# Pre-LN attention and mixture-of-experts block: value projection and second half of routing moved, scores, maxima and exponentials ahead of gate, up and tanh in each step

## The chip, the cores and the metric

One core of a Trainium2 chip. The metric is device time in microseconds (us), here the median of 3 runs. All engines of the core take part: PE (TensorE), ACT (ScalarE), DVE (VectorE), POOL (GpSimd) and SP (SyncE, which only issues DMAs).

## What is computed

A transformer block on x of 32 sequences x 256 tokens x 128 channels in fp32. Below, the reference cut to what matters.

```python
x = x + attn(layernorm(x))            # 16 heads of 8; a query at i sees keys i-63 .. i
x = x + ffn(layernorm(x))
# ffn, per token, 16 experts of 64 hidden, 4 groups of 4 experts:
scores = sigmoid(x @ gate_kernel) + gate_bias
group_sum = sum of the two best scores of each group; the best 2 groups are kept
topk_weight, topk_idx = top_k(where(group kept, scores, 0), 4)
topk_weight = topk_weight / (sum(topk_weight) + 1e-20) * 2.5
y = sum over the 4 experts of weight * ((silu(x @ w_gate) * (x @ w_up)) @ w_down)
shared = (silu(x @ sw_gate) * (x @ sw_up)) @ sw_down      # 128 hidden
return y + shared
```

## The kernel before

The 8192 tokens go through in 16 groups of 512 tokens (two sequences of 256, `GB` = 2). The program is a pipeline written out by hand. Time is cut into slots of 8 steps (`STEPS`); a slot is one new group. Every piece of work has a stage number: stage d of group g runs in slot g + d // 8, step d % 8. So stage 28 (`FF`) of group g runs three slots and 4 steps after its LN1. The function `at` says whether a stage falls into a step. Slots 0 to 5 and 16 to 19 are unrolled, slots 6 to 15 run in a loop, two slots per turn.

Each engine has its own instruction list: for each step, the pieces that fall into it, in an order fixed by the code. Engines meet only at semaphores. Nothing reorders the list of an engine but this code.

In a slot in the middle of the run, work of five groups is under way at once:

- Attention. LN1 (stage 0), transposes of x (`XT` 1), Q projection (`QP` 2), V projection (`VP` 3), K projections of the two sequences (`KP` 6, 8). Q and K exist as a high and a low fp32r part; ACT makes the high parts (`q_hi`, `k_hi`), POOL the low parts (`q_lo`, `k_lo`), DVE the differences (`xT_lo`, `qr_lo`, `kr_lo`, `x_lo`). `v_bd` is V laid out by heads, by ACT (`VB` 4, 5).
- Scores (`SC` 8 to 15): PE writes a unit in two halves to PSUM banks 0 and 1 (band mask L979, products L986); DVE takes the negative maximum of each half (`neg_max` L805); ACT makes the exponentials (`probs` L604, eight instructions); in the next step DVE transposes them (`probsT` L754, stage `TR` 9); PE multiplies with V (`PV` 11, L918) into bank 2, ACT copies that out (`o_f`, stage `OE` 14 and 18), PE transposes (`OT`), DVE divides (`o_n` L819), PE transposes again (`ON`), ACT copies (`oT`), PE applies Wo (`OW`), DVE adds x (`H2`).
- LN2 (17, 21), transposes (`XT2`), router logits (`LG` 24). Routing is shared by POOL and DVE: POOL sums pairs of scores (`pair`, step 0), DVE takes group maxima and the two best groups (`gs`, `g8`, `g_out`, `g_in`, step 1), POOL masks the scores (`ms`, step 1), DVE takes the best experts (`m8`, `w_sum`, `m_out`, step 2), POOL makes the weights (`comb`, step 2). PE transposes them in step 3 (`CT` 27), ACT copies `cT`, SP sends them to DRAM and reads them back spread over partitions (`spread`).
- Feed-forward (`FF` 28 to 35, one pair of experts k per step): PE makes gate into bank 4 and up into bank 5 (`gate_up`, lines L876 to L878); ACT makes tanh of the gate (`th` L562) and a copy of it (`gate`); DVE `tu` = (tanh + 1) * up (L793); POOL gate * spread (L468) and `hh` (L471); PE the down projection a step later (`DN` 29, L1060). `gate_up` of the next pair waits for `tu` and for the gate copy, since banks 4 and 5 are used again. The shared expert (`SH` 27, step 3) uses the same banks after pair 7; its tanh is L580, DVE's `fa` L835 and `hs` L839.

PSUM banks 3 and 6 are a ring of two (`RING`) for all projections and transposes: each use takes the next bank and PE waits until the use before the last one has been taken out. The order of the uses follows from the stage numbers and the places EARLY, POST, WEIGHTS, LATE in a step.

The order inside a step before, cut to the two threads:

```python
# PE:   PV, [K0], [V], [LG], FF gate_up(k), SC scores(u), OT, ON, OW, CT, SH, ..., DN
# ACT:  o_f, kr_hi, th_r, FF th(k), gate(k), oT, cT, SH th, late copies, SC exponentials(u), q_hi, k_hi, v_bd
# DVE:  probsT(u-1), [routing 0], [V], OUT, kr_lo, LN1, [routing 1], FF tu(k), [routing 2, 3],
#       max(u) half 0, [routing 4], max(u) half 1, [routing 5], LN2, o_n, H2, SH fa, hs, [routing 6], low parts
```

## Time and profile before

| | us |
|---|---|
| median of 3 runs | 883.22 |
| lowest, highest | 879.14, 885.05 |
| profiled execution, its own time | 882.66 |
| its span in the profile | 880.9 |
| PE busy | 764.8 |
| POOL busy | 616.3 |
| ACT busy | 607.9 |
| DVE busy | 548.1 |

The profiled execution's own time is 1.8 us longer than its span: start and end lie around it. Busy shares are means over filling, the steady middle and draining; a slot can be found in the trace by its LN1 instruction (`ve` L429 on POOL, 16 times). In a timeline row the first number is the start in us from the span's start, the second the duration in us, then engine, line, operation, output<-inputs, xcount of merged instructions, and in brackets how long the engine was idle before and what ended that. The granted clock is TensorE's, 1.00 for 2.4 GHz and 0.50 for 1.2 GHz.

### The profile page before, as it was taken

The page shows a single profiled execution, that of the slowest core. Times are in us where ns is not written, and L with a number is a line of the kernel's source. Part 1 is how long each engine was busy: PE and PEld are TensorE (multiplying, and loading weights), DVE is VectorE, ACT ScalarE, POOL GpSimd, SP SyncE. Part 2 cuts the span into 40 slices and gives each one's busy share as a digit, 9 for nine tenths or more (in the row PEclk, how much of TensorE's full clock was granted, in tenths as well). Part 3 has the DMA queues.
Part 4 walks back from the last instruction along what each step waited for, and adds up shares of the span by engine and source line. Part 5 has one row for each costly group of instructions (what it writes and reads, how often), then busy time and mean ns, then how long its engine had stood idle before and what let it go on. Part 6 is the DMA issues. An engine that isn't in the chain of part 4 may idle for free.

```text
span 880.9 us, 19798 instructions
## 1 busy us (share of the span) xinstructions
PE 764.8 (87%) x5984; PEld 623.5 (71%) x5984; DVE 548.1 (62%) x1751; ACT 607.9 (69%) x1816; POOL 616.3 (70%) x825
## 2 busy tenths in 40 slices
PE   2567789898998989898998989899898989998876
PEld 1455667686877868687787868678786868777665
DVE  3456666767676676767676676766758676664341
ACT  5678677686767768686876868677677868764332
POOL 2525457778686767968686787868677786857666
PEclk9789799999999999999999999999999999999999
DMA  5000022030312103031312204031211303030321
GB/s 143 24 2 25 1 74 61 17 116 15 99 49 86 61 23 124 0 105 40 97 48 64 81 2 119 24 97 48 82 63 31 114 0 105 29 106 29 122 81 42
DMA packets 50738, 53.86 MB, mean 61 GB/s; under 512 B 5632, under 2 KB 31744, under 8 KB 50560
## 3 DMA queue, kind: packets, MB, share of 16 engines
q1 hardware_dynamic: 50688, 53.25, 19.8%
q8 instruction: 24, 0.39, 0.2%
q14 instruction: 26, 0.21, 0.1%
HBM read 44.31 MB, written 4.72 MB: 56 GB/s over the span
## 4 chain that ended last, share of the span: by engine, by line
PE 26%; ACT 21%; issue 21%; DVE 15%; POOL 12%; DMA 2%; POOLq 1%; DVEq 1%; SPq 1%; ACTq 0%
ACT probs L604 10%; POOL gate L468 5%; PE PS L876 5%; PE PS L986 4%; PE PS L878 4%; PE PS L877 4%; ACT v_bd L522 4%; DVE probsT L754 3%; DVE neg_max L805 3%; PE PS L1060 3%; ACT q_hi L522 3%; POOL hh L471 2%; POOL k_lo L460 2%; PE PS L918 2%; ACT th L562 2%
## 5 line engine op out<-in xcount | busy, mean ns | idle before, releaser
L604 ACT ACTIVATE probs<-PS,neg_max 128x96 f32<-128x96 f32 (+1 forms) x1024 | 244.4, 355 | 86.5 <-DVE neg_max L805 86.5
L468 POOL TENSOR_TENSOR gate<-gate,spread 128x512 f32<-128x512 f32 x128 | 163.6, 1278 | 137.9 <-DMA spread<-weights_by_expert 69.3
L754 DVE STREAM_TRANSPOSE probsT<-probs 128x384 f32<-128x384 f32 (+1 forms) x256 | 124.1, 523 | 113.9 <-ACT probs L604 113.9
L471 POOL TENSOR_TENSOR hh<-gate,tu 128x512 f32<-128x512 f32 x128 | 164.4, 1284 | 15.5 <-POOL gate L468 10.4
L1060 PE MATMUL PS<-wd,hh 128*128 128x128 f32 x1024 | 137.0, 277 | 9.7 <-POOL hh L471 9.7
L793 DVE SCALAR_TENSOR_TENSOR tu<-th,PS 128x512 f32<-128x512 f32 x128 | 87.8, 686 | 84.5 <-PE PS L878 58.7
L1060 PEld LDWEIGHTS PS<-wd,hh 128*128 128x128 f32 x1024 | 127.4, 193 | 15.4 <-POOL hh L471 9.8
L876 PE MATMUL PS<-x_hi,w_hi 128*128 128x512 f32 x288 | 130.3, 453 | 4.8 <-DVE tu L793 3.5
L805 DVE TENSOR_REDUCE neg_max<-PS 128x4 f32<-128x384 f32 (+1 forms) x256 | 124.0, 514 | 9.4 <-PE PS L986 7.1
L562 ACT ACTIVATE th<-PS 128x512 f32<-128x512 f32 x128 | 79.5, 621 | 57.7 <-PE PS L878 57.5
L878 PE MATMUL PS<-x_lo,w_hi 128*128 128x512 f32 x288 | 118.6, 412 | 0.0
L877 PE MATMUL PS<-x_hi,w_lo 128*128 128x512 f32 x288 | 118.3, 411 | 0.0
L918 PE MATMUL PS<-probsT,v_bd 128*64 128x96 f32 (+2 forms) x2048 | 107.7, 248 | 0.3 <-DVE probsT L754 0.3
L986 PE MATMUL PS<-k_hi,q_hi 128*128 128x384 f32 (+2 forms) x256 | 107.2, 419 | 0.0
L979 PE MATMUL PS<-band,ident 128*128 128x256 bf16 (+1 forms) x256 | 73.6, 288 | 30.1 <-POOL k_lo L460 12.4
L918 PEld LDWEIGHTS PS<-probsT,v_bd 128*64 128x64 f32 x2048 | 85.7, 139 | 17.9 <-issue 3.2
L460 POOL TENSOR_TENSOR k_lo<-kr_lo,cst 128x256 fp32r<-128x256 f32 x128 | 74.6, 615 | 21.9 <-DVE kr_lo L661 21.9
L450 POOL TENSOR_TENSOR q_lo<-qr_lo,cst 128x256 fp32r<-128x256 f32 x128 | 75.8, 615 | 17.5 <-PE PS L986 11.9
L986 PE MATMUL PS<-k_hi,q_lo 128*128 128x384 f32 (+2 forms) x256 | 85.7, 335 | 0.0
L979 PEld LDWEIGHTS PS<-band,ident 128*128 128x128 bf16 x256 | 25.4, 99 | 85.0 <-issue 63.1
L986 PE MATMUL PS<-k_lo,q_hi 128*128 128x384 f32 (+2 forms) x256 | 85.5, 334 | 0.0
L522 ACT ACTIVATE gate<-PS 128x512 f32<-128x512 f32 x128 | 79.6, 622 | 0.0
(107 smaller groups left out, 1394.2 us busy)
## 6 DMA issues: line engine op xcount, KB each, us to landing
spread<-weights_by_expert SPq DMA_DIRECT2D x256, 128.0 KB, 3.0
X<-x SPq DMA_DIRECT2D x32, 256.0 KB, 3.5
OUT<-H SPq DMA_DIRECT2D x16, 256.0 KB, 3.0
out<-OUT SPq DMA_DIRECT2D x16, 256.0 KB, 3.2
probsT<-w_gu SPq DMA_DIRECT2D x1, 1152.0 KB, 7.8
wd<-w_down SPq DMA_DIRECT2D x1, 512.0 KB, 8.1
weights_by_expert<-cT SPq DMA_DIRECT2D x16, 32.0 KB, 1.6
probsT<-w_att SPq DMA_DIRECT2D x1, 264.0 KB, 3.4
```

Source lines behind the costliest of these rows:

```text
L468: tt(gate2[:, :], gate[:, k % 2, :], spread[:, k % SP_BUFS, :], ALU.mult).then_inc(s_g2, 1)
L471: tt(hh[:, k % 2, :], gate2[:, :], tu[:, k % 2, :], ALU.mult).then_inc(s_h, 1)
L522: return nc.scalar.activation(dst, src, ACT.Copy, **kw)
L604: ins = nc.scalar.activation(probs[:, u % 2, tt, a, j0:KW], PS[:, tt, a * KW + j0:a * KW + KW], ACT.Exp, bias=neg_max[:, tt, a:a + 1])
L754: ins = v_.transpose(probsT[:, b, :, t0 + tt, c0:3, :].rearrange("p g c q -> p g (c q)"), probs[:, u % 2, tt, :, c0 * Q:KW])
L805: v_.tensor_reduce(neg_max[:, tt, :], src[:, :, j0:KW], AX_X, ALU.max, negate=True).then_inc(s_m, 1)
L876: mm(dst, l_hi, r_hi, start=True, stop=False)
L877: mm(dst, l_lo, r_hi, start=False, stop=False)
L878: return mm(dst, l_hi, r_lo, start=False, stop=True)
L918: ins = mm(PS[r0:r0 + 64, 2, c0:c0 + Q * nq], v_bd[:, g.par, b * NQ + kb, a, :, :].rearrange("p k f -> p (k f)"), pt[:, 3 * kb + 2:3 * kb ...
L986: ins = mm(dst[:, :, KW - nk:KW], ql[:, q1 // Q - 1, :, :].rearrange("p v q -> p (v q)"), kl[:, :, q1 - nk:q1], start=False, stop=(kl is k ...
L1060: ins = mm(PS[:, 7, r], hh[:, k % 2, r], wd[:, k, :], start=(k == 0 and n == 0), stop=(k == NP - 1), skip_group_check=True)
```

## The change

Four things are done.

1. The V projection goes from step 3 to step 5 (`VP` 5), the `v_bd` copies to steps 6 and 7 (`VB` 6), the low K parts of the second sequence on POOL from step 2 to step 3 (`KC_LOW`). The copy of `o_f` stands at the end of ACT's step before (`OE` 13) and not at the beginning of the step.
2. The second half of routing: the eight-best instruction `m8` stands between the two maxima of step 2 (place 4) and not at the beginning of that step, the rest behind `o_n` (places 6 and 7).
3. The group mask: `match_replace` writes -2^60 for a chosen group, and POOL subtracts (`g_in` = `gs` - `g_out`), where DVE compared by a `tensor_scalar`. The kept scores are thus multiplied by 2^60, and so is their sum, to which a constant first column of `m8` adds the small term that a `tensor_scalar` added.
4. In every step PE issues the scores ahead of gate and up, ACT the exponentials ahead of tanh and gate copy, DVE the maxima ahead of `tu`.

```diff
@@ -41,15 +41,16 @@
 
 LN1 = 0
 XT = 1
-QP, VP, VB = 2, 3, 4
+QP, VP, VB = 2, 5, 6
 QC = (4, 8)
 QC_LOW = (4, 9)
 KP = (6, 8)
 KC = (7, 10)
+KC_LOW = (7, 11)
 SC = 8
 TR = 9
 PV = 11
-OE = 14
+OE = 13
 OT, ON, OW = 14, 15, 16
 LN2 = 17
 XT2 = 19
@@ -144,8 +145,8 @@
 LOADS, FFN_LOADS = 4, 4
 PREPARE = 4
 ORDER_PER_SLOT = 5
-ROUTING_DVE, ROUTING_POOL = 9, 4
-NO_SCORE, CHOSEN = -3.0e38, 3.0e38
+ROUTING_DVE, ROUTING_POOL = 8, 5
+NO_SCORE, GROUP_IN = -3.0e38, 2.0 ** 60
...
         ms = sb("ms", [P, NT, E + 4])
-        m8 = sb("m8", [P, NT, 8])
+        m8 = sb("m8", [P, NT, 9])
         m_out = sb("m_out", [P, NT, E + 4])
...
-            pool.wait_ge(s_pool, 4)
+            nc.gpsimd.memset(m8[:, :, 0:1], 2e-20 * GROUP_IN).then_inc(s_pool, 1)
+            pool.wait_ge(s_pool, 5)
...
                     for b in range(GB):
-                        g, _ = at(sl, s, KC[b])
+                        g, _ = at(sl, s, KC_LOW[b])
                         if g:
...
                     if g and part == 1:
-                        pool.wait_ge(s_rt, g.n * ROUTING_DVE + 5)
+                        pool.wait_ge(s_rt, g.n * ROUTING_DVE + 4)
+                        tt(g_in[:, :, :], gs[:, :, 0:N_GROUP], g_out[:, :, 0:N_GROUP], ALU.subtract).then_inc(s_rp, 1)
+                        pool.wait_ge(s_rp, n0 + 3)
                         tt(ms[:, :, 0:E].rearrange("p n (g e) -> p n g e", e=4),
                            sc3.rearrange("p n (g e) -> p n g e", e=4),
                            g_in[:, :, :].unsqueeze(3).broadcast_to([P, NT, N_GROUP, 4]), ALU.mult).then_inc(s_rp, 1)
                     if g and part == 2:
-                        pool.wait_ge(s_rt, g.n * ROUTING_DVE + 9)
+                        pool.wait_ge(s_rt, g.n * ROUTING_DVE + 8)
                         tt(kept[:, :, :], ms[:, :, 0:E], m_out[:, :, 0:E], ALU.subtract).then_inc(s_rp, 1)
-                        pool.wait_ge(s_rp, n0 + 4)
+                        pool.wait_ge(s_rp, n0 + 5)
                         tt(comb[:, :, :], kept[:, :, :], w_sum[:, :].unsqueeze(2).broadcast_to(full),
                            ALU.mult).then_inc(s_cb, 1)
...
-                    g, b = at(sl, s, OE, 4, GB)
-                    if g:
-                        act.wait_ge(s_o_ps, g.n * GB + b + 1)
-                        copy(o_f[:, :, :], PS[:, 2, :].rearrange("p (j q) -> p j q", j=2)).then_inc(s_o, 1)
-
-
...
                                              scale=0.5).then_inc(s_taken[side], 1)
-                    g, k = at(sl, s, FF, 1, NP)
-                    if g:
-                        act.wait_ge(s_g, g.n * NF + k + 2)
-                        nc.scalar.activation(th[:, :], PS[:, 4, :], ACT.Tanh, scale=0.5).then_inc(s_th, 1)
-                        copy(gate[:, k % 2, :], PS[:, 4, :]).then_inc(s_gate, 1)
-
...
                     g, u = at(sl, s, SC, 1, NU)
                     if g:
...
                             ins.then_inc(s_p, 1)
+                    g, k = at(sl, s, FF, 1, NP)
+                    if g:
+                        act.wait_ge(s_g, g.n * NF + k + 2)
+                        nc.scalar.activation(th[:, :], PS[:, 4, :], ACT.Tanh, scale=0.5).then_inc(s_th, 1)
+                        copy(gate[:, k % 2, :], PS[:, 4, :]).then_inc(s_gate, 1)
...
+                    g, b = at(sl, s, OE, 4, GB)
+                    if g:
+                        act.wait_ge(s_o_ps, g.n * GB + b + 1)
+                        copy(o_f[:, :, :], PS[:, 2, :].rearrange("p (j q) -> p j q", j=2)).then_inc(s_o, 1)
                     for b in range(GB):
                         g, pair_ = at(sl, s, QC[b], 1, 2)
...
                     for n in range(NT):
-                        ins = v_.match_replace(g_out[:, n, :], g8[:, n, :], gs[:, n, :], CHOSEN)
+                        ins = v_.match_replace(g_out[:, n, :], g8[:, n, :], gs[:, n, :], -GROUP_IN)
                     ins.then_inc(s_rt, 1)
-                elif half == 0 and place == 6:
-                    dve.wait_ge(s_rt, n0 + 4)
-                    v_.tensor_scalar(g_in[:, :, :], g_out[:, :, 0:N_GROUP], CHOSEN, None,
-                                     ALU.is_ge).then_inc(s_rt, 1)
-
-                elif half == 1 and place == 0:
-                    dve.wait_ge(s_rp, g.n * ROUTING_POOL + 3)
+
+                elif half == 1 and place == 4:
+                    dve.wait_ge(s_rp, g.n * ROUTING_POOL + 4)
                     v_.memset(holder[:, :], 0.0)
                     for n in range(NT):
-                        ins = v_.max(m8[:, n, :], ms[:, n, 0:E])
+                        ins = v_.max(m8[:, n, 1:9], ms[:, n, 0:E])
                     ins.then_inc(s_rt, 1)
-                elif half == 1 and place == 1:
+                elif half == 1 and place == 6:
+                    dve.wait_ge(s_rt, n0 + 5)
+                    v_.tensor_reduce(w_sum[:, :], m8[:, :, 0:1 + TOP_K], AX_X, ALU.add)
+                    v_.memset(m8[:, :, 1 + TOP_K:9], NO_SCORE).then_inc(s_rt, 1)
+                elif half == 1 and place == 7:
                     dve.wait_ge(s_rt, n0 + 6)
-                    v_.tensor_reduce(w_sum[:, :], m8[:, :, 0:TOP_K], AX_X, ALU.add)
-                    v_.memset(m8[:, :, TOP_K:8], NO_SCORE).then_inc(s_rt, 1)
-                elif half == 1 and place == 2:
-                    dve.wait_ge(s_rt, n0 + 7)
-                    v_.tensor_scalar(w_sum[:, :], w_sum[:, :], 2e-20, None, ALU.add)
+                    v_.memset(holder[:, :], 0.0)
                     for n in range(NT):
-                        ins = v_.match_replace(m_out[:, n, :], m8[:, n, :], ms[:, n, :], 0.0)
+                        ins = v_.match_replace(m_out[:, n, :], m8[:, n, 1:9], ms[:, n, :], 0.0)
                     ins.then_inc(s_rt, 1)
-                elif half == 1 and place == 3:
-                    dve.wait_ge(s_rt, n0 + 8)
                     v_.reciprocal(w_sum[:, :], w_sum[:, :]).then_inc(s_rt, 1)
...
                                 probs[:, u % 2, tt, :, c0 * Q:KW])
                         ins.then_inc(s_pt, 1)
 
-                    routing(sl, s, 0)
-
...
                         stats(sl, X[:, g.par, :, :], NT, st1, mv1).then_inc(s_mv1, 1)
-                    routing(sl, s, 1)
-                    g, k = at(sl, s, FF, 1, NP)
-                    if g:
-                        dve.wait_ge(s_th, g.n * NF + k + 2)
-                        dve.wait_ge(s_u, g.n * NF + k + 2)
-                        v_.scalar_tensor_tensor(tu[:, k % 2, :], th[:, :], 1.0, PS[:, 5, :], ALU.add,
-                                                ALU.mult).then_inc(s_tu, 1)
                     routing(sl, s, 2)
                     routing(sl, s, 3)
                     g, u = at(sl, s, SC, 1, NU)
...
                         routing(sl, s, 4 + tt)
+                    g, k = at(sl, s, FF, 1, NP)
+                    if g:
+                        dve.wait_ge(s_th, g.n * NF + k + 2)
+                        dve.wait_ge(s_u, g.n * NF + k + 2)
+                        v_.scalar_tensor_tensor(tu[:, k % 2, :], th[:, :], 1.0, PS[:, 5, :], ALU.add,
+                                                ALU.mult).then_inc(s_tu, 1)
                     g, b = at(sl, s, LN2, 4, GB)
                     if g:
...
                                          ALU.mult).then_inc(s_taken[side], 1)
+                    routing(sl, s, 6)
                     g, b = at(sl, s, OW, 4, GB)
                     if g:
                         side, bank = filled(dve, sl, s, POST)
...
                                          X2[:, g.par, 2 * b:2 * b + 2, :], ALU.add).then_inc(s_taken[side], 1)
+                    routing(sl, s, 7)
                     g, _ = at(sl, s, SH)
                     if g:
                         f = g.n * NF + 1
...
                                                 ALU.mult).then_inc(s_tu, 1)
-                    routing(sl, s, 6)
-
                     keys(1)
...
                         ins.then_inc(s_filled[side], 1)
-
-                    g, k = at(sl, s, FF, 1, NP)
-                    if g:
-                        gate_up(g, k, k + 1)
 
                     g, u = at(sl, s, SC, 1, NU)
...
                             ins.then_inc(s_s, 1)
 
+                    g, k = at(sl, s, FF, 1, NP)
+                    if g:
+                        gate_up(g, k, k + 1)
+
                     g, b = at(sl, s, OT, 4, GB)
                     if g:
                         side, bank = free(POST)
```

The rest of the diff on ACT is the block from the tanh of `FF` to the copies of `XT2`, moved as it is behind the exponentials.

Where the rows of the program stand now. All rows below are from slot 16, where they stand without register instructions between them; the slots before have the same order and, in steps 0 to 3, also LN1 and the projections of a new group. First ACT, step 1 to the beginning of step 2, before: `th` and `gate` are tanh and copy of the gate, `probs` the exponentials.

```order
L562 ACTIVATE th<-PS 128x512
L522 ACTIVATE gate<-PS 128x512
L604 ACTIVATE probs<-PS,neg_max 128x96 x8
L522 ACTIVATE q_hi<-qr_hi,cst 128x8x32 x2
L522 ACTIVATE o_f<-PS 128x512
L562 ACTIVATE th<-PS 128x512
```

ACT at the same place now:

```order
L565 ACTIVATE probs<-PS,neg_max 128x96 x8
L572 ACTIVATE th<-PS 128x512
L526 ACTIVATE gate<-PS 128x512
L526 ACTIVATE o_f<-PS 128x512
L526 ACTIVATE q_hi<-qr_hi,cst 128x8x32 x2
L565 ACTIVATE probs<-PS,neg_max 128x96 x8
L572 ACTIVATE th<-PS 128x512
```

Tanh and gate copy of a step stood ahead of its exponentials and now stand behind them; `o_f` stands ahead of the `q_hi` copies. Next DVE, step 2, before: `m` and `w_sum` are routing, `tu` the feed-forward, `neg_max` the maxima.

```order
L754 STREAM_TRANSPOSE probsT<-probs 128x4x96 x2
L710 MEMSET holder 128x1
L712 MAX m<-ms 128x8 x4
L716 TENSOR_REDUCE w_sum<-m 128x4
L717 MEMSET m 128x4x4
L793 SCALAR_TENSOR_TENSOR tu<-th,PS 128x512
L720 TENSOR_SCALAR w_sum<-w_sum 128x4
L722 MATCH_REPLACE m_out<-m,ms 128x20 x4
L726 RECIPROCAL w_sum<-w_sum 128x4
L805 TENSOR_REDUCE neg_max<-PS 128x4 x2
L818 RECIPROCAL o_rs<-PS 128x32
L819 TENSOR_TENSOR o_n<-PS,o_rs 128x256
```

DVE, step 2, now:

```order
L750 STREAM_TRANSPOSE probsT<-probs 128x4x96 x2
L792 TENSOR_REDUCE neg_max<-PS 128x4
L708 MEMSET holder 128x1
L710 MAX m<-ms 128x8 x4
L792 TENSOR_REDUCE neg_max<-PS 128x4
L799 SCALAR_TENSOR_TENSOR tu<-th,PS 128x512
L811 RECIPROCAL o_rs<-PS 128x32
L812 TENSOR_TENSOR o_n<-PS,o_rs 128x256
L714 TENSOR_REDUCE w_sum<-m 128x4
L715 MEMSET m 128x4x4
L718 MEMSET holder 128x1
L720 MATCH_REPLACE m_out<-m,ms 128x20 x4
```

The maxima moved ahead of `tu` with `m` between them, the rest of routing moved behind `o_n`, and the `tensor_scalar` of `w_sum` is gone.

## Rows read from the trace of the kernel before

**Rows 1.** The page, busy us (share) xinstructions, and the chain by engine.

```profile
PE 764.8 (87%) x5984; PEld 623.5 (71%) x5984; DVE 548.1 (62%) x1751; ACT 607.9 (69%) x1816; POOL 616.3 (70%) x825
PE 26%; ACT 21%; issue 21%; DVE 15%; POOL 12%; DMA 2%; POOLq 1%; DVEq 1%; SPq 1%; ACTq 0%
```

**Rows 2.** Timeline, POOL, the first LN1 instruction of slots 4 and 15.

```profile
147.52 0.20 POOL L429 TENSOR_TENSOR ve<-mv,eps 128x4 f32<-128x4 f32 x1 [2.50 <-DVE mv L675]
...
703.10 0.20 POOL L429 TENSOR_TENSOR ve<-mv,eps 128x4 f32<-128x4 f32 x1 [2.47 <-DVE mv L675]
```

**Rows 3.** Stretches: length, busy PE, PEld, DVE, ACT, POOL, clock, DMA, GB/s.

```profile
350.73:401.52 50.79, 46.87 (x376) 38.49 (x376) 34.23 (x109) 37.38 (x114) 38.42 (x52) 0.97 0.20 62
401.52:450.73 49.21, 45.29 (x376) 37.50 (x376) 33.96 (x109) 37.38 (x114) 38.45 (x51) 1.00 0.21 65
366.00:368.20 2.20, 0.00 (x0) 0.00 (x0) 2.12 (x9) 1.14 (x6) 2.20 (x4) 1.00 0.00 0
369.60:372.60 3.00, 3.00 (x11) 1.98 (x9) 1.78 (x4) 1.99 (x5) 1.94 (x4) 0.50 0.00 0
```

**Rows 4.** Waits over the whole span: us in total, times, longest us.

```profile
DVE probsT L754 <- ACT probs L604: 113.9, 116, 2.1
ACT probs L604 <- DVE neg_max L805: 86.5, 74, 3.0
POOL gate L468 <- DMA spread<-weights_by_expert: 69.3, 16, 6.0
...
PE PS L876 <- DVE o_n L819: 36.5, 13, 3.0
```

**Rows 5.** Timeline, ACT and DVE, an ordinary step, and the spacing of `probsT`.

```profile
419.82 1.04 DVE L754 STREAM_TRANSPOSE probsT<-probs 128x384 f32<-128x384 f32 x2 [0.25 <-ACT probs L604]
...
420.78 0.67 DVE L766 STREAM_TRANSPOSE v_keys<-PS 128x512 f32<-128x512 f32 x1
...
433.04 0.64 ACT L562 ACTIVATE th<-PS 128x512 f32<-128x512 f32 x1
...
433.71 0.69 DVE L793 SCALAR_TENSOR_TENSOR tu<-th,PS 128x512 f32<-128x512 f32 x1 [1.16 <-ACT th L562]
...
434.32 1.01 DVE L805 TENSOR_REDUCE neg_max<-PS 128x4 f32<-128x384 f32 x2
434.90 1.96 ACT L604 ACTIVATE probs<-PS,neg_max 128x96 f32<-128x96 f32 x8 [0.74 <-DVE neg_max L805]
...
436.71 0.95 ACT L522 ACTIVATE q_hi<-qr_hi,cst 128x256 fp32r<-128x256 f32 x2
```

**Rows 6.** Timeline, steps 0 to 3 of slot 9: LN1, routing, V projection, shared expert.

```profile
401.52 0.20 POOL L429 TENSOR_TENSOR ve<-mv,eps 128x4 f32<-128x4 f32 x1 [2.47 <-DVE mv L675]
...
404.76 1.30 POOL L468 TENSOR_TENSOR gate<-gate,spread 128x512 f32<-128x512 f32 x1
...
407.46 0.32 POOL L498 TENSOR_TENSOR sc<-th_r,bias 128x64 f32<-128x64 f32 x1
...
408.54 0.25 DVE L686 TENSOR_REDUCE gs<-pair 128x16 f32<-128x96 f32 x1 [1.20 <-POOL pair L503]
...
412.30 0.20 POOL L477 TENSOR_TENSOR ve<-mv,eps 128x2 f32<-128x2 f32 x1
...
414.39 0.30 POOL L506 TENSOR_TENSOR ms<-sc,g_in 128x64 f32<-128x64 f32 x1
...
419.03 0.50 PE L876 MATMUL PS<-xT_hi,w_hi 128*128 128x512 f32 x1 [2.90 <-DVE o_n L819]
...
423.11 0.48 PE L876 MATMUL PS<-x_hi,w_hi 128*128 128x512 f32 x1
...
424.72 0.69 DVE L835 SCALAR_TENSOR_TENSOR fa<-th,PS 128x512 f32<-128x512 f32 x1 [1.21 <-ACT th L580]
```

**Rows 7.** The two `tensor_scalar` lines: duration in ns min/median/max, first and last start.

```profile
L705 DVE TENSOR_SCALAR g_in<-g_out x16: 142/1044/1058, 109.4 to 839.6; 128x16 f32<-128x16 f32 x16
L720 DVE TENSOR_SCALAR w_sum<-w_sum x16: 161/529/569, 112.7 to 842.2; 128x4 f32<-128x4 f32 x16
```

More of the change, by code:

```diff
@@ L423, in slot @@
                                                 ALU.add).then_inc(s_pool, 1)
-                        pool.wait_ge(s_pool, 5)
+                        pool.wait_ge(s_pool, 6)
                     g, _ = at(sl, s, LN1)
@@ L558, in slot @@
                                              scale=0.5).then_inc(s_taken[side], 1)
+                    g, u = at(sl, s, SC, 1, NU)
+                    if g:
+                        j0 = Q if u % 4 == 0 else 0
+                        if u >= 2 or not (g.fixed and g.n == 0):
+                            act.wait_ge(s_pt, g.n * NU + u - 1)
+                        for tt in range(2):
+                            act.wait_ge(s_m, 2 * (g.n * NU + u) + tt + 1)
+                            for a in range(HG):
+                                ins = nc.scalar.activation(
+                                    probs[:, u % 2, tt, a, j0:KW], PS[:, tt, a * KW + j0:a * KW + KW], ACT.Exp,
+                                    bias=neg_max[:, tt, a:a + 1])
+                            ins.then_inc(s_p, 1)
                     g, k = at(sl, s, FF, 1, NP)
@@ L595, in slot @@
                         copy(x2_hi[:, g.par, T * b:T * b + T], bank[:, 0:T]).then_inc(s_high[side], 1)
-                    g, u = at(sl, s, SC, 1, NU)
+                    g, b = at(sl, s, OE, 4, GB)
                     if g:
-                        j0 = Q if u % 4 == 0 else 0
-                        if u >= 2 or not (g.fixed and g.n == 0):
-                            act.wait_ge(s_pt, g.n * NU + u - 1)
-                        for tt in range(2):
-                            act.wait_ge(s_m, 2 * (g.n * NU + u) + tt + 1)
-                            for a in range(HG):
-                                ins = nc.scalar.activation(
-                                    probs[:, u % 2, tt, a, j0:KW], PS[:, tt, a * KW + j0:a * KW + KW], ACT.Exp,
-                                    bias=neg_max[:, tt, a:a + 1])
-                            ins.then_inc(s_p, 1)
+                        act.wait_ge(s_o_ps, g.n * GB + b + 1)
+                        copy(o_f[:, :, :], PS[:, 2, :].rearrange("p (j q) -> p j q", j=2)).then_inc(s_o, 1)
                     for b in range(GB):
```

## The prediction, made before the changed kernel ran

> **What bounds the kernel now.** I read the page's busy shares and chain first: TensorE (PE) is busy 87% of the span, yet the chain that ended last spends only 26% on it and hops between PE, ACT, DVE and POOL [rows 1]. So no engine is full; hand-overs set the pace. Next, how long one slot (8 steps, 512 tokens) takes: the first LN1 instruction of slot 4 starts at 147.52, that of slot 15 at 703.10 [rows 2], 555.6 us for 11 slots, 50.5 us each. Two neighbouring slots by stretches [rows 3]: one of 50.79 us with a granted clock of 0.97, one of 49.21 with 1.00; PE is busy 46.87 and 45.29, DVE only 34, POOL 38, ACT 37. The difference, 1.58 us, is a stretch at a granted clock of 0.5 (1.2 GHz instead of 2.4), which most slots have: the one shown, 369.6 to 372.6, comes right behind one in which PE did nothing, 366.0 to 368.2. The table of waits says who waits [rows 4]: PE's V projection for `o_n` 36.5 us in 13 times, so 2.9 per slot; DVE's `probsT` for the exponentials 113.9; the exponentials for the maxima 86.5; POOL's gate product 69.3 for the spread weights.
>
> Within a step [rows 5] the reader should see that tanh and exponentials are two separate threads now. Tanh `th` (433.04) waits only for PE, DVE's `tu` follows it at once (433.71), then the maxima (434.32), then the exponentials (434.90). The next tanh does not need them: whatever DVE does behind the maxima is covered by 1.8 us of exponentials.
>
> **V projection two steps later.** In step 3 its PSUM bank is the one that `o_n` is being read from the wait of 2.90 at 419.03 [rows 6]; in step 5 that bank has long been released. Its own instructions are the same, only elsewhere. That takes away 2.9 us of PE time per slot and with it the idle stretch ahead of the slow clock, up to 1.6 more. But this is a gain only if PE remains what a slot waits for. The `v_bd` copies on ACT move from steps 4, 5 to 6, 7 and `k_lo` of the second sequence on POOL from step 2 to 3, each beside a wait: I cost both at 0, and 1.2 to 2.3 us on their engine if that cover is gone. The copy of `o_f` now stands at the end of the step before; it waits for the PV products that PE issues first in its next step, and what queues behind it on ACT (two `q_hi` copies, then the exponentials) has about 2 us of room.
>
> **Routing.** Two `tensor_scalar` instructions leave DVE. They are tiny (128x16 and 128x4), but take 1.04 and 0.53 us in the median and 0.14 and 0.16 at their shortest [rows 7]. Gone: 1.6 us per slot. The Trainium skill (SBUF — State Buffer, Who interferes with whom) says that `tensor_scalar` can enter a mode that takes the port pair shared with GpSimd, and then fully blocks behind a GpSimd instruction; the trace agrees. By that rule the full 1.6 us return; if another DVE instruction took over the blocking, 0.3 would, and a slot would be 1.3 longer than I say. The rows of the sum take 1.6. POOL gets one `tensor_tensor` of 128x16 instead: between 0 and the 0.30 of `ms` [rows 6]; I take 0.25.
>
> **Scores, maxima, exponentials ahead of gate, up, tanh.** This is the part that decides. All queues run in order. ACT now issues tanh(k) behind exponentials(u), DVE issues `tu`(k) behind tanh(k), everything else of DVE's step behind `tu`(k), then `probsT`(u) and maximum(u+1) of the next step, and only those release exponentials(u+1). The two threads have become one ring, DVE to ACT to DVE, eight times per slot. Its length from rows:
> - ACT's part of a step, from the end of the first maximum to the start of `tu`: hand-over 0.07, exponentials 1.81 (434.90 to 436.71), tanh 0.64, hand-over 0.03, together 2.55 [rows 5]; eight times 20.4.
> - DVE's part is all it does in a slot, 33.96 us [rows 3], less the second maximum of each step, which runs beside the exponentials (8 x 0.5, half of the 1.01 of two in rows 5), less the 1.6 of the two `tensor_scalar`: 28.4.
> - The shared expert's gate in step 3: now its PSUM bank is free only after `tu`(7), and from its matmuls' start to DVE's `fa` there are 1.6 us (423.11 to 424.72) [rows 6].
> That makes 50.4. Then two waits of DVE for POOL lie in the ring, both ahead of a maximum:
> - `gs` in step 1 waits for `pair`. From POOL's first LN1 instruction to `gs` the trace has 7.0 us (401.52 to 408.54: LN1 3.2, gate and hidden products 2.7, sums 1.1) [rows 6]. In that time the ring does maximum 0.4, ACT 2.5, `tu` 0.6, two of 128x256 at 0.4 (an estimate: half of `tu`'s 128x512), `probsT` of a narrow step 0.7: some 4.8. Wait 2.2.
> - `m8` in step 2, now between the two maxima, waits for `ms`. Behind the exponentials of step 1 come 1.8 + 1.1 (tanh, gate copy), POOL's products 2.7, LN2 2.1 (412.30 to 414.39), `g_in` and `ms` 0.6, hand-overs 0.1: 8.4. The ring needs 2.55 + 0.6 + LN2 statistics and `xT_lo` 0.7 each (estimated by `tu`'s 0.69) + `probsT` 0.96 (419.82 to 420.78) + 0.5 = 6.0. Wait 2.4. Before, this gate copy stood ahead of the exponentials, and POOL alone set `ms`.
> Sum per slot: 50.4 + 2.2 + 2.4 = 55.0 us. Walking the eight steps through on all five queues, with spacings as in rows 5 and 6, gave 55 as well, nearly all of the excess in steps 0 to 3; PE then waits some 10 us per slot, and the spread weights arrive before POOL wants them, so the DMA wait of rows 4 goes. Bounds for a slot: 50.4 if both POOL waits vanish; 57 if in addition no hand-over is as short as assumed.
>
> **Clock.** Long PE waits in step 3 (for `comb`, then for `tu`(7) ahead of the shared gate) stand where a slow stretch follows: before it was a wait of 2.9 [rows 6], now several with little between them. A slow stretch cost 1.58 when PE was the bound. Now part of it falls on PE's slack: I take 1.0 per slot, from 0 (none) to 3.2 (two, at full price). The skill (TensorE: Matmul & The Clock Gate, HAM oscillation) describes a kernel that is throttled in every iteration by its waits; by that rule no slot escapes, where 2 of the 11 slots now seem to.
>
> **Sum,** against the profiled execution's own 882.66 us. Slots 4 to 15 have both threads: 12 x (55.0 − 50.5) = +54. Slot 16 has no LN1 and no projections: +2. Clock +12. Filling (slots 0 to 3): one of the 13 V waits, −3 (from −15 to +5, since exponentials no longer wait for late copies there). Draining: the shorter routing chain, −1. Together +64: 946.7; the median of the runs is 883.22, 0.56 above the profiled one, so 947.
>
> **Rivals.**
> 1. *PE remains the bound.* The waits go and nothing takes their place: a slot is PE's busy 45.3 [rows 3], 12 x 5.2 = 62 less, some 820. For it: PE is at 87%. Against it: it needs the ring to be under 45.3, and its DVE and ACT terms alone are 48.8. If only the V wait and its clock go, 12 x 3.9 = 47 less, some 836. Together 13%. It decides from the point where DVE and ACT together need less than PE in a slot.
> 2. *The ring is there, but without POOL waits*, because POOL, too, is re-timed by the later order: 50.4 per slot, nothing gained or lost: about 880. For it: POOL is busy 38 of 50.8. Against it: the chain behind `gs` is POOL's own work back to back. 5%.
> 3. *The slow clock becomes the rule*: two slow stretches in each slot and all of it on the ring, 3.2 instead of 1.0: 12 x 2.2 = 26 more, 973. 12%.
> 4. My forecast, around 947: 70%.
>
> **How the numbers follow.** The likeliest case gives 947. Its own range is from 905 (POOL waits half as long and no slow clock: 55.0 − 2.3 − 50.5 = 2.2 per slot, +26 − 4) to 970. The range for 8 times in 10 reaches from 903 to 976: it takes in rival 3 and leaves out rivals 1 and 2 (18%) and little else. Faster by over 1%: 0.13 (rival 1). Within 1%, about what a measurement of this kernel can tell from no change: 0.05. Slower: 0.82.
>
> **What would show it.** In the profile after: the interval between LN1 instructions 54 to 57 us instead of 50.5; PE's V projection no longer waiting for `o_n` (right in any case); `probsT` hardly waiting for exponentials, as it now comes after `tu`; instead DVE's `tu` waiting for tanh some 2 us in every step, a new large row; `gs` and `m8` waiting over 2 us each; PE waiting for `tu` ahead of the shared expert's gate; POOL waiting for ACT's gate copy, not for DMA. I am wrong if `tu` waits little and PE's busy share rises over 87%; the mechanism is right and its size wrong if those waits are there and the slot is under 53 us.

## The result, and the profile after

| | before | after |
|---|---|---|
| median (range), us | 881.18 (877.65 to 885.05) | 971.83 (971.25 to 972.43) |
| profiled execution, its own time | 882.66 | 971.25 |
| its span | 880.9 | 969.5 |
| mean granted clock over the span | 0.954 | 0.900 |

The changed kernel is slower: ratio 1.103, 95% interval 1.097 to 1.108. The forecast was 947 in 903 to 976. The direction and the range held; the time came out 25 us above the forecast.

The page of the changed kernel, its busy us (share) and instructions, and the row of the granted clock in 40 slices:

```profile
PE 811.1 (84%) x5984; PEld 672.3 (69%) x5984; DVE 519.1 (54%) x1735; ACT 601.1 (62%) x1816; POOL 622.2 (64%) x842
PEclk8899989988879989798998888998897999989999
```

The same row of the kernel before:

```profile
PEclk9789799999999999999999999999999999999999
```

Beside [rows 1] no engine became fuller: PE's share fell by 3 points, DVE's and ACT's by 7 or 8. PE's busy time rose by 46 us with the same 5984 instructions. That is the clock: 18 of the 40 slices stand at 7 or 8 tenths, against 3 before, and the same matmul lasts longer.

The LN1 instructions of slots 4 and 15 (timeline, POOL):

```profile
139.32 0.20 POOL L431 TENSOR_TENSOR ve<-mv,eps 128x4 f32<-128x4 f32 x1 [0.48 <-DVE mv L677]
...
773.40 0.20 POOL L431 TENSOR_TENSOR ve<-mv,eps 128x4 f32<-128x4 f32 x1 [0.42 <-DVE mv L677]
```

634.1 us for 11 slots, 57.6 each, against 50.5 from [rows 2]. So the 88.6 us by which the span grew (969.5 against 880.9) fall into three parts: filling, up to the first row, 8.2 less; the 11 slots 78.5 more; from slot 15's LN1 to the end 196.1 against 177.8, 18.3 more.

The table of stretches of the same kernel (length, busy PE, PEld, DVE, ACT, POOL, clock, DMA share, GB/s): the 11 slots, one of them, and two pieces of its step 3.

```profile
139.32:773.40 634.08, 554.31 (x4120) 465.61 (x4121) 353.36 (x1188) 406.27 (x1245) 427.18 (x572) 0.89 0.18 56
485.19:542.59 57.40, 48.08 (x370) 40.09 (x369) 31.74 (x108) 36.85 (x113) 38.85 (x52) 0.92 0.17 55
...
508.95:511.85 2.90, 0.00 (x0) 0.00 (x0) 0.78 (x2) 2.90 (x11) 1.75 (x4) 0.66 0.00 0
512.50:517.50 5.00, 5.00 (x32) 4.26 (x30) 2.70 (x5) 0.98 (x2) 2.82 (x4) 0.58 0.22 77
```

The first row is the one to compare with the kernel before. The same 11 slots of before:

```profile
147.52:703.10 555.58, 512.41 (x4116) 422.17 (x4116) 375.07 (x1199) 411.82 (x1244) 422.86 (x562) 0.97 0.21 64
```

PE ran the same matmuls for 554.3 us instead of 512.4. It was idle for 79.8 us instead of 43.2. The last two rows show where: PE does nothing for 2.90 us, and in the five us from 512.50 on the granted clock is 0.58 on average, so most of them are at 1.2 GHz. With the two levels 1.00 and 0.50, a mean clock c over a stretch of length s means 2 x (1 − c) x s at half clock. That is 12.7 us in a slot of after and 3.0 in one of before.

The table of waits of the changed kernel (us in total, times, longest), whole span:

```profile
ACT probs L565 <- DVE neg_max L792: 252.6, 140, 4.2
DVE tu L799 <- ACT th L572: 185.3, 98, 2.1
POOL gate L470 <- ACT gate L526: 181.0, 66, 7.7
...
PE PS L869 <- DVE tu L799: 48.5, 30, 3.0
...
DVE m L710 <- issue: 41.1, 15, 4.3
...
DVE gs L688 <- POOL pair L505: 24.1, 15, 3.4
PE PS L869 <- DVE x_lo L663: 21.7, 15, 2.6
```

Against [rows 4]: the wait of ACT's exponentials for the maxima has tripled from 86.5, and DVE's `tu` waits 1.9 us for tanh in most steps, 185.3 us in all; before, the same row of the table was 24.2 us in 29 times. These are the two halves of one ring: ACT waits for DVE, DVE waits for ACT. POOL's wait for the spread weights has gone down from 69.3 to 8.8 and is replaced by one for ACT's gate copy. The wait of the V projection for `o_n` is gone. The last row nobody had forecast: the router logits now wait for `x_lo` (0.2 us in the whole run before).

Now one slot's waits, timeline of the changed kernel, steps 1 to 3 of the slot that starts at 485.19:

```profile
492.22 0.25 DVE L688 TENSOR_REDUCE gs<-pair 128x16 f32<-128x96 f32 x1 [2.47 <-POOL pair L505]
...
493.40 1.96 ACT L565 ACTIVATE probs<-PS,neg_max 128x96 f32<-128x96 f32 x8 [4.16 <-DVE neg_max L792]
...
501.83 0.17 DVE L710 MAX8 m<-ms 128x8 f32<-128x16 f32 x1 [2.62 <-issue]
...
508.05 0.99 DVE L792 TENSOR_REDUCE neg_max<-PS 128x4 f32<-128x384 f32 x2
508.61 1.96 ACT L565 ACTIVATE probs<-PS,neg_max 128x96 f32<-128x96 f32 x8 [1.80 <-DVE neg_max L792]
510.41 0.65 ACT L572 ACTIVATE th<-PS 128x512 f32<-128x512 f32 x1
...
511.09 0.69 DVE L799 SCALAR_TENSOR_TENSOR tu<-th,PS 128x512 f32<-128x512 f32 x1 [2.05 <-ACT th L572]
...
511.91 0.79 PE L869 MATMUL PS<-x_hi,w_hi 128*128 128x512 f32 x1 [2.98 <-DVE tu L799]
```

From the start of the maxima (508.05) the reader can follow the ring by eye: exponentials 508.61, tanh 510.41, `tu` 511.09, and only then PE's shared gate at 511.91. In [rows 5] tanh stood ahead, and `tu` (433.71) ahead of the maxima (434.32). The two waits of DVE for POOL are there at 2.47 and 2.62 us in this slot; over the run they are 24.1 us in 15 times and 41.1 in 15, so 1.6 and 2.7 on average. The second one says "issue", so the profile names no releaser; but by the program `m` waits for the product `ms`, and `ms` ends at 501.79 (501.49 + 0.30), 0.04 us ahead of it.

### The profile page after: what moved, and what is told of

Its sections match the earlier page's. It is cut to its first block and busy times, and to the rows that moved or that the text cites. A ratio compares the mean times of both kernels' runs of the same rounds, so it can differ in the third digit from the quotient of the medians.

```text
span 969.5 us, 19809 instructions
## 1 busy us (share of the span) xinstructions
PE 811.1 (84%) x5984; PEld 672.3 (69%) x5984; DVE 519.1 (54%) x1735; ACT 601.1 (62%) x1816; POOL 622.2 (64%) x842
## 5 line engine op out<-in xcount | busy, mean ns | idle before, releaser
L565 ACT ACTIVATE probs<-PS,neg_max 128x96 f32<-128x96 f32 (+1 forms) x1024 | 246.4, 347 | 252.7 <-DVE neg_max L792 252.6
L799 DVE SCALAR_TENSOR_TENSOR tu<-th,PS 128x512 f32<-128x512 f32 x128 | 87.9, 687 | 241.5 <-ACT th L572 185.3
L869 PE MATMUL PS<-x_hi,w_hi 128*128 128x512 f32 x288 | 134.0, 465 | 49.8 <-DVE tu L799 48.5
L1053 PE MATMUL PS<-wd,hh 128*128 128x128 f32 x1024 | 147.0, 290 | 9.7 <-POOL hh L473 9.7
L1053 PEld LDWEIGHTS PS<-wd,hh 128*128 128x128 f32 x1024 | 138.0, 206 | 17.1 <-POOL hh L473 10.2
L750 DVE STREAM_TRANSPOSE probsT<-probs 128x384 f32<-128x384 f32 (+1 forms) x256 | 122.7, 518 | 10.7 <-ACT probs L565 10.4
L870 PE MATMUL PS<-x_hi,w_lo 128*128 128x512 f32 x288 | 127.1, 441 | 0.0
L871 PE MATMUL PS<-x_lo,w_hi 128*128 128x512 f32 x288 | 126.8, 440 | 0.0
L911 PE MATMUL PS<-probsT,v_bd 128*64 128x96 f32 (+2 forms) x2048 | 110.0, 252 | 2.9 <-DVE probsT L750 2.8
L869 PEld LDWEIGHTS PS<-x_hi,w_hi 128*128 128x128 f32 x288 | 61.8, 215 | 70.5 <-DVE tu L799 33.4
L911 PEld LDWEIGHTS PS<-probsT,v_bd 128*64 128x64 f32 x2048 | 88.0, 142 | 21.3 <-DVE probsT L750 4.8
L526 ACT ACTIVATE gate<-PS 128x512 f32<-128x512 f32 x128 | 82.0, 640 | 0.0
```

Source lines behind the costliest of these rows:

```text
L565: ins = nc.scalar.activation(probs[:, u % 2, tt, a, j0:KW], PS[:, tt, a * KW + j0:a * KW + KW], ACT.Exp, bias=neg_max[:, tt, a:a + 1])
L750: ins = v_.transpose(probsT[:, b, :, t0 + tt, c0:3, :].rearrange("p g c q -> p g (c q)"), probs[:, u % 2, tt, :, c0 * Q:KW])
L869: mm(dst, l_hi, r_hi, start=True, stop=False)
L870: mm(dst, l_lo, r_hi, start=False, stop=False)
L871: return mm(dst, l_hi, r_lo, start=False, stop=True)
L911: ins = mm(PS[r0:r0 + 64, 2, c0:c0 + Q * nq], v_bd[:, g.par, b * NQ + kb, a, :, :].rearrange("p k f -> p (k f)"), pt[:, 3 * kb + 2:3 * kb ...
```

## The experiments

Twelve kernels, each timed beside the kernel before on the same chip; ratios are to that, with a 95% interval. Three sets were run, and the median of the kernel before was 883.70, 879.64 and 879.71 us in them, so a difference of a few us between kernels of different sets says little. The names: "b" starts from the kernel before, "a" from the changed one. The "slot" is the distance between the LN1 instructions of slots 4 and 15, divided by 11.

| | median us (range) | ratio | slot us |
|---|---|---|---|
| b_v_only | 852.72 (851.84 to 854.01) | 0.966 (0.963 to 0.969) | 48.7 |
| b_order_only | 985.80 (984.41 to 990.64) | 1.119 (1.115 to 1.123) | 57.9 |
| a_ff_first | 857.96 (852.18 to 861.50) | 0.970 (0.965 to 0.976) | 49.0 |
| a_pe_old | 1037.71 (1036.35 to 1041.01) | 1.175 (1.172 to 1.178) | 62.3 |
| a_act_ff | 852.25 (849.48 to 857.55) | 0.966 (0.962 to 0.971) | 48.8 |
| a_rt1_early | 934.12 (932.28 to 935.02) | 1.061 (1.056 to 1.065) | 54.2 |
| a_warm | 959.58 (956.71 to 961.48) | 1.089 (1.084 to 1.095) | 56.0 |
| a_old_all | 813.63 (812.83 to 814.65) | 0.923 (0.919 to 0.927) | 46.0 |
| a_old_oe | 815.22 (814.73 to 816.27) | 0.926 (0.923 to 0.929) | 46.0 |
| a_old_rt | 861.42 (858.68 to 865.71) | 0.978 (0.974 to 0.981) | 49.7 |
| a_old_v | 834.52 (834.32 to 835.24) | 0.948 (0.945 to 0.951) | 47.0 |
| a_v_back | 971.87 (967.00 to 973.16) | 1.103 (1.098 to 1.108) | 56.9 |

### Two parts of the change, each alone

**b_v_only**: the kernel before with the V projection moved, nothing else.

```diff
-QP, VP, VB = 2, 3, 4
+QP, VP, VB = 2, 5, 6
```

> The kernel before with only the V projection and the v_bd copies moved (VP, VB = 5, 6). My theory: in the kernel before PE is what a slot waits for in step 3, so the 2.9 us wait for o_n and the slow clock behind it both go: 12 slots x (2.9 to 4.5), 830 to 850 us. Rival (the wait only moves, another wait takes its place in steps 3 and 4): 875 to 885 us.

31 us come back alone, less than the 35 to 54 of 12 slots x (2.9 to 4.5): 852.72 lies just outside the expected 830 to 850. The stretch of its 11 slots:

```profile
140.35:676.29 535.94, 503.94 (x4116) 412.89 (x4116) 374.78 (x1199) 409.51 (x1244) 423.27 (x561) 1.00 0.22 66
```

The granted clock is 1.00, so the wait took the slow stretch along. Something else then holds PE, in the table of waits of this kernel:

```profile
PE PS L979 <- ACT probs L604: 28.4, 27, 1.8
```

PE's scores wait for the exponentials that still occupy banks 0 and 1; before, this row was 10.5 us in 13 times.

**b_order_only**: the kernel before with only the in-step order changed, on PE, DVE and ACT.

```diff
 # ACT
+  SC: exponentials(u)
   FF: tanh(k), gate(k)
   ...
-  SC: exponentials(u)
 # DVE
-  FF: tu(k)
   SC: max(u) half 0, half 1
+  FF: tu(k)
 # PE
-  FF: gate_up(k)
   SC: scores(u)
+  FF: gate_up(k)
```

> The kernel before with only the order inside the steps changed (scores, maxima, exponentials ahead of gate, up and tanh on PE, DVE and ACT); V projection and routing stay as they were. Ring theory: the whole loss is here, and with the V wait still there and m8 ahead of both maxima it is 960 to 1000 us. Rival (the loss comes from where V or the second half of routing was put): 875 to 895 us.

The order alone costs 102 us, in 57.9 us slots: more than the whole change. `tu` waits 196.7 us for tanh in 103 times, as in the changed kernel. So the loss is the order's, and the rest of the change (V, `k_lo`, `o_f` and routing together) gives 14 us back.

### The order, engine by engine

**a_ff_first**: the changed kernel with gate, up, tanh and `tu` back ahead of scores, maxima and exponentials on all three engines. The late copies of ACT (`x_hi`, `k_hi` and their like) stay behind the exponentials, where the change has them.

> The changed kernel with gate_up, tanh and gate copy, and tu put back ahead of scores, exponentials and maxima; V, routing, o_f and the late copies behind the exponentials stay as changed. Ring theory: tanh no longer waits for the exponentials, PE is the bound again and has no V wait: 815 to 845 us. Rival (V, routing or the late copies cause the loss): over 950 us.

114 us come back, but not all that was expected (857.96 against 815 to 845). Two waits of PE in this kernel's table show where some of the rest is:

```profile
DVE x_lo L663 <- ACT x_hi L526: 31.6, 16, 2.2
...
PE PS L869 <- DVE x_lo L663: 16.0, 15, 2.6
PE PS L1032 <- ACT oT L526: 15.8, 14, 1.6
```

The copy `x_hi` behind the exponentials is late for `x_lo`, and PE's router logits wait for that; the copy `oT` is late for the transposes of LN2 (L1032), which need its bank. a_old_all below, in which only these late copies are ahead again, is 44 us faster, and there the logits wait 0.3 us in all and L1032 not at all. That the late copies cost 44 us is shown; the two waits make up 31.8 us of it, and how the rest comes about is not shown.

**a_act_ff**: the changed kernel with one edit on ACT alone; PE and DVE keep their new order.

```diff
 # ACT
+  FF: tanh(k), gate(k)
   SC: exponentials(u)
-  FF: tanh(k), gate(k)
```

> The changed kernel with ACT's order alone put back: tanh and gate copy ahead of the exponentials; PE still issues the scores first and DVE the maxima first. Ring theory: the ring is cut where tanh stood behind the exponentials, and one engine's order suffices: 855 to 895 us (the exponentials now wait for gate and up, which PE issues 1.3 us later than before). Rival (every one of the three orders costs its share): 930 us or more.

This is the run that tells the ring apart from everything else. With one engine's order undone the ring is open, since DVE's `tu`(k) finds its tanh done, and 120 us are back, at 852.25 slightly more than the 855 to 895 expected. PE (84% busy after) and DVE (54%) still run their new order. The main waits of this kernel:

```profile
ACT th L560 <- PE PS L871: 196.1, 103, 4.5
...
ACT probs L571 <- DVE neg_max L792: 34.0, 37, 2.3
```

Tanh now waits for PE's gate, so PE is what is late. The exponentials' wait for the maxima has fallen from 252.6 to 34.0, and `tu` is no longer among the large waits for tanh.

**a_pe_old**: the changed kernel with PE's order alone undone: `gate_up`(k) again ahead of scores(u).

> The changed kernel with PE's order alone put back (gate_up ahead of the scores); ACT and DVE stay as changed. Ring theory: the ring runs over ACT and DVE only, PE's order hardly matters: 960 to 985 us. Rival (scores ahead of gate and up on PE cause the loss, since gate and up then come late for tanh): under 900 us.

The theory that PE's order hardly matters (960 to 985) fell, and its rival (under 900) too: 1037.71, 66 us slower still. A step of this kernel, timeline:

```profile
509.35 0.69 DVE L799 SCALAR_TENSOR_TENSOR tu<-th,PS 128x512 f32<-128x512 f32 x1 [1.85 <-ACT th L572]
...
510.17 0.49 PE L869 MATMUL PS<-x_hi,w_hi 128*128 128x512 f32 x1 [0.23 <-DVE tu L799]
...
511.70 0.42 PE L979 MATMUL PS<-k_hi,q_hi 128*128 128x384 f32 x1
...
512.51 1.22 DVE L792 TENSOR_REDUCE neg_max<-PS 128x4 f32<-128x384 f32 x2 [0.80 <-PE PS L979]
513.10 1.96 ACT L565 ACTIVATE probs<-PS,neg_max 128x96 f32<-128x96 f32 x8 [2.08 <-DVE neg_max L792]
```

`gate_up` needs the banks that `tu` frees, so it starts at 510.17. The scores stand behind it in PE's queue, and the maxima behind the scores. PE has become the third member of the ring: its six gate and up matmuls, 1.5 us from 510.17 to 511.70, now lie between `tu` and the next maxima. The maxima wait 134.0 us for PE in this kernel's table of waits. Given the new order on ACT and DVE, PE had to follow; that part of the change repairs 66 us of the damage.

### Where the ring waits

**a_rt1_early**: POOL makes the group mask and `ms` ahead of its gate product of step 1, and not behind it.

```diff
 # POOL, step 1
+  RT: g_in, ms
   FF: gate * spread, hh
   LN2
-  RT: g_in, ms
```

> The changed kernel with POOL's mask of the scores (g_in, ms) ahead of the gate product in step 1 instead of behind LN2, so that m8 has nothing to wait for. If the m8 wait of 2.6 us lies in the ring as predicted: 971.8 - 12 x 2.6 = 941 us (932 to 952). Rival (it is slack, or the gs wait and PE take its place): 964 to 974 us.

37.7 us come back, 3.5 per slot. (DVE's memset ahead of `m` writes a scratch tile of its own in this kernel.) The wait of `m` disappears from the table, and that of `gs` stays: `DVE gs L693 <- POOL pair L517` has 24.0 us in 15 times, as in the changed kernel. So a wait of DVE for POOL in the ring costs at least its full length: `m` waited 2.7 us on average. What the slot gained beyond that, 0.8 us, came with a clock of 0.94 in place of 0.89 over the 11 slots; that the clock is the cause was not tried.

**a_warm**: in step 3 PE does matmuls whose result is not used, where it would wait for `comb` and for `tu`.

```diff
 # PE, step 3
+  7 matmuls into unused partitions of the bank
   wait for comb, transposes of comb
+  16 of the same
   SH: gate, up
```

> The changed kernel with idle matmuls added on PE in step 3, 7 ahead of the wait for comb and 16 ahead of the shared expert's gate, into partitions of the bank that nobody reads (their results are not used). They fill the two waits and, if it is these waits that slow the clock, no slow stretch follows. If the slow clock costs what the slots are longer than my sum (57.6 - 55.0 = 2.6 us): 941 us (930 to 955). Rival (slow stretches fall on PE's slack, my sum is off elsewhere): 965 to 980 us.

12 us come back: 959.58 lies between the two theories (930 to 955, and 965 to 980) and in neither range. The stretch of the 11 slots:

```profile
142.04:757.89 615.85, 567.36 (x4369) 466.79 (x4369) 350.97 (x1189) 405.56 (x1245) 427.03 (x572) 0.95 0.19 58
```

The clock rose from 0.89 to 0.95, so half clock fell from 12.7 to 5.6 us per slot, and the slot from 57.6 to 56.0. That is 0.23 us of slot for each us at half clock that goes. If the rest were worth the same, all 12.7 would be worth some 2.9 us, and a slot at full clock would take 54.7. This is an estimate beyond what was run, and the added matmuls may have cost something themselves.

### What the rest of the change is worth outside the ring

**a_old_all**: the changed kernel with the whole in-step order of before, the late copies ahead of the exponentials among it. V projection and routing stay as changed; `o_f` stands behind the exponentials.

> The changed kernel with the whole order inside the steps put back on PE, DVE and ACT, the late copies ahead of the exponentials too; V, k_lo, o_f and routing stay as changed. Against a_ff_first (858) it tells what the late copies behind the exponentials are worth, against b_v_only (852.7) what routing and o_f are worth. If the rest of the change is neutral: 848 to 858 us. Rival (routing and o_f gain another 1.5 us per slot): 830 to 840 us.

The best of all: 0.923 of the time before, 158 us below the changed kernel, and faster than both the expectation (848 to 858) and its rival (830 to 840). The stretches, 11 slots and one:

```profile
135.38:640.95 505.57, 494.82 (x4116) 413.70 (x4116) 357.03 (x1188) 411.09 (x1244) 424.33 (x572) 1.00 0.23 70
411.04:457.02 45.98, 44.98 (x376) 37.60 (x376) 32.43 (x108) 37.36 (x114) 38.55 (x52) 1.00 0.23 70
```

PE is busy 98% of this time, at full clock, and POOL, the next, 84%. Now PE does bound the kernel, and in the slot shown its one wait over 0.9 us is 1.00 for `comb`.

**a_old_oe**: the same with `OE` back at 14 and `o_f` at the beginning of the step.

> a_old_all with the copy of o_f back at the beginning of ACT's step (OE = 14). In the kernel before PE waited 18.8 us in 29 times for o_f in front of the transposes; if the move of that copy is what took this away, the run is 14 to 22 us slower than a_old_all (813.6): 828 to 836. Rival (the copy's place is worth nothing, all of the 39 us between b_v_only and a_old_all are routing): 811 to 817.

1.6 us, within 0.2% of a_old_all: the place of `o_f` is worth nothing that matters.

**a_old_rt**: a_old_all with the routing of before: its place, and the two `tensor_scalar`.

> a_old_all with routing as in the kernel before (m8 and what follows at the beginning of step 2, both tensor_scalar on DVE, no subtraction on POOL); V, k_lo and o_f stay moved. If routing stood ahead of the maxima of step 2 and so on PE's way to the next scores: 828 to 842 us. By my prediction's price (only the 1.6 us of the two tensor_scalar per slot, and only where DVE is the bound, which it is not here): 811 to 818.

47.8 us slower than a_old_all, where 15 to 30 were expected. Timeline of this kernel, step 2:

```profile
451.68 0.17 DVE L713 MAX8 m<-ms 128x8 f32<-128x16 f32 x1 [0.81 <-issue]
...
452.29 0.69 DVE L794 SCALAR_TENSOR_TENSOR tu<-th,PS 128x512 f32<-128x512 f32 x1
452.89 1.16 DVE L721 TENSOR_SCALAR w_sum<-w_sum 128x4 f32<-128x4 f32 x1
...
454.86 1.02 DVE L806 TENSOR_REDUCE neg_max<-PS 128x4 f32<-128x384 f32 x2
455.46 1.96 ACT L601 ACTIVATE probs<-PS,neg_max 128x96 f32<-128x96 f32 x8 [3.82 <-DVE neg_max L806]
...
456.55 0.28 PE L980 MATMUL PS<-band,ident 128*128 128x256 bf16 x1 [1.78 <-ACT probs L601]
```

From `m` (451.68) to the maxima (454.86) DVE needs 3.2 us, of which 2.5 are routing. ACT is idle 3.82 for it, and PE's next scores wait 1.78 for the exponentials, 39.9 us in 28 times over the span. Moving routing behind the maxima takes exactly this chain away. How the 48 us divide between the place and the two `tensor_scalar` was not tried, but the trace has a part of it: the `tensor_scalar` at 452.89 takes 1.16 us of the chain, and over the run its median is 1.20 us where it was 0.53 in [rows 7]. With `k_lo` moved out of step 2, POOL runs its gate product (452.74 to 454.03) at that moment, and the `tensor_scalar` ends with it, at 454.05. b_v_only, which is this kernel with `k_lo` and `o_f` where they were, has a median of 0.53 for it and takes 852.72 us, 8.7 less (ratios 0.966 and 0.978): beside the old routing these two moves together are a loss.

**a_old_v**: a_old_all with the V projection back in step 3.

> a_old_all with the V projection back in step 3 (VP, VB = 3, 4). b_v_only says that its place is worth 31 us: then 840 to 850. Rival: its wait is for o_n, which in the kernel before stood behind routing and the maxima of step 2 on DVE and now stands ahead of most of it, so the wait has gone with routing: 813 to 822.

20.9 us slower than a_old_all, between the 840 to 850 that b_v_only suggested and the 813 to 822 of the rival. The wait for `o_n` is back, but only 12.9 us in 11 times where it was 36.5 in [rows 4]: in the new routing most of DVE's routing work of step 2 stands behind `o_n` and no longer ahead of it.

**a_v_back**: the changed kernel, its order too, with the V projection back in step 3.

> The changed kernel with the V projection back in step 3. Ring theory: PE waits in step 3 anyway, so V's place is worth little there: 968 to 985 us (it puts V ahead of the scores of step 3, which can delay maximum and exponentials). Rival (the 31 us of b_v_only add up with everything else): 1000 us or more.

971.87 against 971.83: the place of V is worth nothing there, although PE waits for `o_n` again, 53.1 us in 14 times. The parts do move: filling is 8.3 us longer (first LN1 of slot 4 at 147.65 instead of 139.32), the slot 0.7 shorter (56.94 instead of 57.64), 7.7 us in 11 slots. So the equal totals are in part luck: two effects of some 8 us cancel. The shorter slot goes with a higher clock over the 11 slots, 0.93 instead of 0.89, although PE is idle longer in them.

## Why the prediction came out as it did

**Right: the ring.** Against the prediction's own list: the slot is 57.6 us, just above the 54 to 57 named; V does not wait for `o_n`; `probsT` hardly waits for the exponentials (10.4 us in place of 113.9); `tu` waits 1.9 us for tanh; `gs` and `m` wait 2.47 and 2.62 in the slot shown where 2.2 and 2.4 were worked out, though the ring's own terms ahead of `gs` add up to 5.0 and not to the 4.8 written, so to a wait of 2.0, and over the run `gs` waits only 1.6 on average, under the 2 us named as a sign, and `m` 2.7; PE waits 2.98 for `tu` ahead of the shared gate and is idle 7.3 us per slot in all (79.8 in 11), where some 10 were worked out; POOL waits for the gate copy and not for DMA. That it is the ring, and not one of these waits by itself, is shown by a_act_ff: one engine's order undone, and the kernel is faster than before. b_order_only shows it from the other side. Rival 2, a ring without POOL waits, is out; a_rt1_early shows that without one of the two a slot takes 54.2, where the sum without it gives 52.6 and rival 2 has 50.4. Rival 1 was wrong for this kernel because the ring takes longer than PE's work of a slot; but its number, some 820, is near what the kernel does with the whole old order (813.63). That nearness is partly luck: of the waits that go, rival 1 had only V's in its account, worth 20.9 us there, and no price for routing, worth 47.8.

**The sum was 25 us short: three of its terms were mis-sized.** The mechanism held. The terms:

- *"I take 1.0 per slot, from 0 (none) to 3.2"* for the clock. A slot measured 57.6 against the 55.0 of the sum without the clock, so 2.6 are left for it if the rest of the sum was right; a_warm's trend puts it at 2.9. That makes 11 x 1.6 = 18 more than forecast. The prediction saw one or two slow stretches of 3 us per slot; there are 12.7 us at half clock. Rival 3 was nearer in size for this term (3.2). Only the 12 us of a_warm are shown; the rest is the difference between a measured slot and a sum. The tie of a slow stretch to one wait is also loose: V waits 2.7 to 3.0 us in all 11 slots of the kernel before, and two of them, the one with the 2.90 of [rows 6] among them, run at 1.00 all the same; and in the slot that [rows 3] shows slowed, 1.4 us of matmuls lie between the empty stretch (to 368.20) and the slow one (from 369.60), so the slow one does not come right behind it.
- *"Slot 16 has no LN1 and no projections: +2."* From slot 15's LN1 on the run is 18.3 us longer where the sum allows 4.5 + 1 + 2 − 1 = 6.5. By DVE's `OUT` additions, one per slot: from slot 15's LN1 to its own 38.0 us instead of 31.9, from there to that of slot 16 55.5 instead of 46.7, so 14.9 longer in two slots; the next two spacings are 2.9 and 1.8 longer, the last 1.3 shorter. The ring runs on in slot 16, for which only +2 was allowed, since it has no LN1 and no projections.
- *"Filling (slots 0 to 3): one of the 13 V waits, −3"*. It is −8.2, and the V projection accounts for it: moved alone, it brings the first LN1 of slot 4 forward by 7.2 us from the kernel before (147.52 to 140.35, b_v_only), by 8.3 in the changed kernel (147.65 in a_v_back, 139.32) and by 9.0 with the old order (144.35 in a_old_v, 135.38 in a_old_all). The change without V moves nothing there: 147.65 in a_v_back against 147.52.

Together 18 + 12 − 5 = 25.

**Two reasons that were wrong though the sum hardly felt it.** Routing was priced at the 1.6 us per slot of its two `tensor_scalar`. In the kernel bound by PE it is worth 47.8 us, 3.8 per slot (49.7 against 46.0), since what counts is not DVE's time but what stands behind it: maxima, exponentials, PE's scores. The 1.6 were also too little for the two instructions themselves where `k_lo` has moved: 1.03 and 1.20 us in the median of a_old_rt. And late copies of ACT behind the exponentials had no price; in the changed kernel the logits wait 21.7 us for `x_lo`, and with the ring open the place of all these copies costs 44 us (a_ff_first against a_old_all).

**Effects do not add.** V's place is worth 31 us in the kernel before (b_v_only), 21 beside the new routing (a_old_v) and nothing in the ring (a_v_back). So the waits do not add up: what a removed wait is worth depends on the next one behind it.

On how to look for the bound: the Trainium skill (Perfetto Trace Analysis, Identifying the Most-Contended Engine) says to optimize the engine with the highest occupancy first; for TensorE it does not trust the busy share of the matmuls and looks at that of the weight loads. In the changed kernel PE comes first either way, with 84% by its matmuls and 69% by its weight loads (PEld), against POOL's 64%. Yet the wait on PE that a_v_back adds changes nothing, while one edit on ACT, at 62%, gives 120 us. Here the measurement decides: the ranking by occupancy does not find the bound of a kernel in which two queues wait for each other.

**What stays open.** DVE's order alone was not undone: `tu` would then stand ahead of the maxima and wait for a tanh that stands behind the exponentials, which wait for those maxima, and nothing would move. The price of the slow clock beyond what a_warm took away is not shown, nor what in the 2.6 us per slot beyond the sum is clock and what is error of the sum. Of routing's 47.8 us, place and instructions were not separated.

## What to carry to other kernels

Before an order within a step is changed on several engines, write down for each queue what stands behind the instruction that waits, and follow it until it returns: two threads that shared DVE and ACT, with tanh never behind the exponentials, became one ring here, 8 times per slot, with all engines under 85%. Keep the short link that the other thread depends on (tanh and `tu`) ahead of the long one, and if a ring must be, keep third parties' waits out of it (a_rt1_early: 3.5 us per slot for one wait). A wait is worth its length only where it lies on what bounds the kernel, so time each part of a change alone: this one without its new order beats the kernel before by 7.7%.
